# Query products between the tiles of the first stage: an order of instructions on three engines is changed

## What is computed

```python
def layernorm(x): return (x - mean(x)) / sqrt(var(x) + 1e-5)

# attention with a summed key-value product
h = layernorm_wb(layernorm(X))
Q, K, V = split(h @ W_in + b_in, 3)              # W_in: 512 x 1536
Q, K = rope_half(Q), rope_half(K)                # first 256 features rotated
A = sum over tokens of (K / norm(K)) * V         # one row of 512 per batch
x = X + layernorm(((A * Q) @ W_out + b_out) + layernorm(X))

# feed-forward: 2 of 8 experts per token, and a shared one
n = layernorm(x)
routed = sum over the token's top 2 of gate * (gelu(n @ w1[e] + b1[e]) @ w2[e] + b2[e])
shared = gelu(n @ shared_w1 + shared_b1) @ shared_w2 + shared_b2
out = x + layernorm(routed + shared)
```

## Time and profile before

| | |
|---|---|
| time, median of 3 runs | 949.71 us (947.07 to 954.91) |
| time of the profiled execution | 945.85 us |
| its span, first to last instruction | 944.0 us |
| TensorE (PE) busy | 93% of the span |
| VectorE (DVE) busy | 67% |
| ScalarE (ACT) busy | 46% |
| GpSimd (POOL) busy | 41% |
| granted TensorE clock, mean | 0.984 of 2.4 GHz |
| first stage, first product of group 1 to `sum_acc(1)` | 54.47 to 305.53 us |

### The profile page before, as it was taken

How to read it: one execution, slowest core, us unless ns; L and a number is a source line. 1 busy time by engine, 2 the same in 40 slices (tenths; PEclk the granted TensorE clock), 3 DMA queues, 4 the chain that set the end, 5 groups by cost and what they waited for, 6 DMA issues and landing times.

```text
span 944.0 us, 14783 instructions
## 1 busy us (share of the span) xinstructions
PE 879.7 (93%) x4558; PEld 724.0 (77%) x4558; DVE 636.5 (67%) x1370; ACT 436.1 (46%) x829; POOL 390.0 (41%) x321
## 2 busy tenths in 40 slices
PE   4999999999999989999999987799999999998986
PEld 3788777877888667777877776688888888886865
DVE  6866976966966765666656587366665556564877
ACT  5235445245243142241222544366666666664564
POOL 1456557366454000000000000467777567762175
PEclk9999999999999999999999998799999999999998
DMA  8327977878558895568433889497888878787999
GB/s 302 113 92 263 333 253 263 318 261 312 212 194 332 343 340 217 200 235 288 150 112 120 331 333 274 102 234 138 148 148 165 202 145 164 149 132 179 360 190 212
DMA packets 87626, 209.03 MB, mean 221 GB/s; under 512 B 11496, under 2 KB 19944, under 8 KB 82432
## 3 DMA queue, kind: packets, MB, share of 16 engines
q1 hardware_dynamic: 62592, 162.29, 47.5%
q0 software_dynamic: 19360, 43.60, 25.2%
q10 hardware_dynamic: 5600, 2.20, 1.0%
HBM read 117.05 MB, written 91.01 MB: 220 GB/s over the span
## 4 chain that ended last, share of the span: by engine, by line
PE 47%; DVE 10%; issue 10%; ACT 4%; POOL 3%; DMA 2%; DVEq 0%; POOLq 0%; ACTq 0%
PE bank L1822 3%; PE bank L1807 3%; PE bank L1820 3%; PE bank L1821 3%; PE bank L1837 3%; PE bank L1578 3%; PE bank L1839 3%; PE bank L1838 3%; PE bank L1579 3%; PE bank L1580 3%; PE bank L1829 2%; PE bank L1573 2%; PE bank L1728 2%; PE bank L1729 2%; PE bank L1730 2%
## 5 line engine op out<-in xcount | busy, mean ns | idle before, releaser
L1527 POOL DMA_INDIRECT f_scratch<-ro,dst x71 | 112.5, 1585 | 56.9 <-issue 19.8
L1519 POOL DMA_INDIRECT xr<-n_scratch,ids x71 | 70.1, 987 | 75.8 <-issue 54.8
L1578 PE MATMUL bank<-wkv_hi,h_hi 128*128 128x512 f32 x248 | 97.2, 392 | 0.0
L1580 PE MATMUL bank<-wkv_hi,h_lo 128*128 128x512 f32 x248 | 96.6, 389 | 0.0
L1579 PE MATMUL bank<-wkv_lo,h_hi 128*128 128x512 f32 x248 | 96.5, 389 | 0.0
L1319 DVE TENSOR_TENSOR ro<-bank,b2b 128x512 f32<-128x512 f32 x71 | 49.2, 692 | 68.3 <-PE bank L1839 55.4
L1820 PE MATMUL bank<-we,x_hi 128*128 x284 | 86.0, 303 | 0.3 <-DVE x_lo L1299 0.3
L1822 PE MATMUL bank<-we,x_lo 128*128 x284 | 80.5, 283 | 0.0
L1821 PE MATMUL bank<-we,x_hi 128*128 x284 | 80.3, 283 | 0.0
L633 ACT ACTIVATE sq<-kb 128x512 f32<-128x512 f32 x32 | 20.3, 633 | 125.8 <-DVE kb L946 125.8
L1837 PE MATMUL bank<-we,g_hi 128*128 x142 | 56.8, 400 | 3.2 <-DVE g_lo L1311 2.3
(11 more groups left out here) (242 smaller groups left out, 2523.6 us busy)
## 6 DMA issues: line engine op xcount, KB each, us to landing
xg<-in_X SPq DMA_DIRECT2D x15, 1024.0 KB, 7.9
we<-expert_scratch SPq DMA_DIRECT2D x6, 2048.0 KB, 13.1
w_lo<-in_w SPq DMA_DIRECT2D x16, 512.0 KB, 5.3
expert_scratch<-w_hi SPq DMA_DIRECT2D x16, 512.0 KB, 2.9
expert_scratch<-w_lo SPq DMA_DIRECT2D x16, 512.0 KB, 4.2
q_scratch<-qh SPq DMA_DIRECT2D x8, 1024.0 KB, 3.9
q_scratch<-qb SPq DMA_DIRECT2D x8, 1024.0 KB, 6.1
q_hi<-q_scratch SPq DMA_DIRECT2D x8, 1024.0 KB, 4.8
```

Of the source, the lines that this page charges most:

```text
L1519: pool.indirect_dma_start(xr[u][:, :], None, n3_dram, bass.IndirectOffsetOnAxis(ids[:, i:i + 1], 0)).then_inc(row_in[u], 16)
L1527: pool.indirect_dma_start(f_dram, bass.IndirectOffsetOnAxis(dst[:, i:i + 1], 0), ro[i % NRO][:, :], None, compute_op=ALU.add).then_inc(r_s ...
L1578: pe.matmul(dst, hi(k), w_hi(k), start=(k == 0), stop=False)
L1580: last = pe.matmul(dst, lo(k), w_hi(k), start=False, stop=(k == KD - 1 and not more))
```

## The change

Groups 1 to 7 get a new order; group 0 keeps the old one.

- TensorE: `q(g, j)` stands behind the keys and values of tile j. Both `turn` pairs of the next group stand around `q(g, 2)`, so ahead of the fourth tile.
- ScalarE: `bias_q(g, (j,))` stands in the loop over tiles, behind `norm_k(g, j)` and a `unit_hi` for each tile. `front_split` of all four slices stands behind the third tile's bias.
- GpSimd: `q_times_sin` and `front_lo(g + 1)` stand ahead of the fourth tile's `rnorm` and the last two accumulates.
- The lists of VectorE and SyncE are as before.

```diff
@@ bias_q
-                    if m in (1, 2):
-                        unit_hi_in(g, 1 + m)
@@ ScalarE
                     norm_k(g, j)
                     if j == 1 and g >= 1:
                         q_hi_parts(g - 1)
-                    if j % 2 == 0:
-                        unit_hi_in(g, j // 2)
-                if g + 1 < NG:
-                    front_split(g + 1, (g + 1) % 2, (0, 1))
-                    bias_q(g, (0,))
-                    front_split(g + 1, (g + 1) % 2, (2, 3))
-                    bias_q(g, (1, 2, 3))
+                    unit_hi_in(g, j)
+                    if g >= 1:
+                        bias_q(g, (j,))
+                        if j == 2 and g + 1 < NG:
+                            front_split(g + 1, (g + 1) % 2)
+                if g == 0:
+                    front_split(1, 1, (0, 1))
+                    bias_q(0, (0,))
+                    front_split(1, 1, (2, 3))
+                    bias_q(0, (1, 2, 3))
@@
-            act.wait_ge(tp_full, KD * NG)
-            bias_q(NG - 1)
             q_hi_parts(NG - 1)
@@ GpSimd
-                rnorm(g, 3)
-                accumulate(g, 2)
-                accumulate(g, 3)
-                if g + 1 < NG:
-                    front_lo(g + 1)
-                q_times_sin(g)
+                if g == 0:
+                    rnorm(g, 3)
+                    accumulate(g, 2)
+                    accumulate(g, 3)
+                    front_lo(1)
+                    q_times_sin(0)
+                else:
+                    q_times_sin(g)
+                    if g + 1 < NG:
+                        front_lo(g + 1)
+                    rnorm(g, 3)
+                    accumulate(g, 2)
+                    accumulate(g, 3)
@@ TensorE
                 for j in range(GT):
                     kv(g, j, 0)
-                    if j == GT - 1 and g + 1 < NG:
+                    if g == 0 and j == GT - 1:
+                        turn(1, (0, 1))
+                    kv(g, j, 1)
+                    if g == 0:
+                        continue
+                    if j == 2 and g + 1 < NG:
                         turn(g + 1, (0, 1))
-                    kv(g, j, 1)
+                    q(g, j)
+                    if j == 2 and g + 1 < NG:
+                        turn(g + 1, (2, 3))
                 if g == 0:
+
                     pe.wait_ge(w_split, 3 * KD)
-                for m in range(KD):
-                    q(g, m)
-                    if m == 0 and g + 1 < NG:
-                        turn(g + 1, (2, 3))
+                    for m in range(KD):
+                        q(g, m)
+                        if m == 0:
+                            turn(1, (2, 3))
```

## The result

The changed kernel takes 966.36 us (964.40 to 968.24, median of 4) where the kernel before takes 948.39 on the same occasions: a ratio of 1.0186, 95% interval 1.0152 to 1.0220. It is slower by 18 us; the forecast was 6.1 slower, 955.8, and its range ended at 965. The profiled executions differ by as much: 964.40 against 945.85.

The account below looks back on a forecast made before the run. TensorE, busy 93% of the span, was taken as the bound. Six groups at 37.04 plus 0.81, 32.65 and 1.5 give 257.2 us against 251.06: 949.7 + 6.1 = 955.8 us, range 948 to 965.

Parts of the forecast that it names:

- Query products between the tiles: First stage: each query buffer is asked for again after three or more products, so the 5.1 us bias wait goes.
- The second turned pair: Ahead of the fourth tile TensorE waits for ScalarE's read-out of rows 0 and 1: 2.62 us in each of six groups.
- The clock, rival C: A product behind each of six holds runs at 1.2 GHz, 2.72 us more each: +16 on top, 972; chance 0.03.
- Weight units: ScalarE's third unit is through at T+23.8, ahead of bias_q(g, 2) at 25.57; inside the sum it costs nothing.
- rival A: Weight loads decide through a VectorE, SyncE and ScalarE loop of 35.3 to 37.0, or 39 with collisions: 964; chance 0.16.
- End of the stage: Before sum_acc(1), one query product instead of four follows the last keys and values: 1.4 us wait, 0.1 restart.
- Rival B: The second turned pair finds its banks free, so groups take 34.42: -9.6 us, 940; chance 0.05.

Follow-up runs that it names:

- experiment 4: The changed kernel with group 7 alone back in the old order (four keys-and-values tiles, then four query products) on three engines: 960.12 us, ratio 1.0120.
- experiment 1: The changed kernel with nine extra matmuls a group, result overwritten, filling TensorE's waits around the second turned pair: 961.48 us, ratio 1.0135.
- experiment 3: The changed kernel with the third weight unit's high part moved on ScalarE behind the bias and all four rows' read-out: 963.88 us, ratio 1.0155.
- experiment 2: The changed kernel with the next group's first two rows read out on ScalarE ahead of the third weight unit and bias: 949.00 us, ratio 1.0004.
- experiment 5: The kernel of experiment 2 with the fourth weight unit's high part moved on ScalarE behind the fourth bias and the acol copy: 945.13 us, ratio 0.9951.
- experiment 7: The changed kernel with TensorE's second turned pair moved from behind q(g, 2) to behind kv(g, 3, 0): 950.01 us, ratio 1.0019.

## Why the prediction was wrong

The path was right and its size was not: +6.1 forecast, +18.0 measured. By its steps:

*Query products between the tiles.* Right: no wait for `q_free` in groups 1 to 4 and 6. But the step overlooked that `sum_acc(0)` takes a query bank in turn. Between `q(4, 3)` and `q(5, 0)`, which then share a bank, stand two large products and not three or more.

*The second turned pair.* Right in place and in size: 2.62 worked out; group 1, where nothing else happened, took 37.08 for 37.04, and without the hold two groups took 34.45 and 34.43 for 34.42.

*The clock, rival C.* This is the step that failed most: the cost of a fall of the clock behind the holds stood in the sum at nothing. It had a chance of 0.03 because "the old gaps of 1.1 and 0.7 left the granted clock at 1.00". Those are single gaps of at most 1.1; the hold has 2.2 us of idle with 0.6 of transposes between. (Whether the sum or the 1.54 alone matters, no run separates.) Four falls behind holds and one behind the last accumulate: the first product behind the four took 3.43, 4.41, 4.42 and 3.93 where 2.84 was forecast, 4.8 together. With 0.7 for the slowed transposes of groups 2 and 6, and the 1.3 by which the stages behind are longer, it is 6.8 in the profile (behind the fifth fall the first product takes 4.21, and 2.96 in experiment 4, which has no fall there); experiment 1 measures 4.9 less in the median. The price was wrong too, at 2.72 for each of six. Five of twelve holds of exactly 1.54 and 0.67 (in the changed kernel and experiments 3 and 4) have a fall behind them, and one costs 0.9 to 1.6. The kernel before had a comparable hold all along, in group 0 (idle 1.45 and 0.61 at 43.90 and 45.14), the same in every kernel here. The window of 40 to 50 us, before and in experiment 2:

```profile
40.00:50.00 10.00, 7.94 (x39) 6.18 (x38) 5.27 (x8) 5.65 (x10) 7.02 (x7) 1.00 0.36 133
```
```profile
40.00:50.00 10.00, 7.93 (x33) 6.16 (x32) 5.38 (x8) 5.57 (x10) 7.02 (x8) 0.83 0.39 140
```

Unchanged code, and one execution has the fall and the other hasn't; of the ten profiles six have it and four don't. A single profile with a clock of 1.00 doesn't show that an idle time is free.

*Weight units.* "Inside the sum it costs nothing" failed as a term. The slack was 1.8 us. The loads landed later than 5.2 (median 6.2 in this stage of the changed kernel), and in group 2 VectorE came to `k_tile(1)` at T+12.7 instead of T+11.1. In group 2 ScalarE waits for it with the bias behind it:

```profile
118.00 1.06 ACT L677 ACTIVATE w_hi<-w_lo 128x1024 fp32r<-128x1024 f32 x1 [3.46 <-DMA w_lo<-in_w]
118.97 0.67 ACT L646 ACTIVATE qb<-bank,bq 128x512 f32<-128x512 f32 x1
```

That put 0.9, 0.2 and 1.1 on the holds of groups 2, 3 and 4 (2.45, 1.78 and 2.64 instead of 1.54), 2.3 together; experiment 3, without them, is 2.5 faster in the median, which agrees but, at its scatter, doesn't fix the size. It is rival A's queue, but not rival A: no loop set the period. Of the fourth unit's wait the prediction said that "queued behind it is only `bias_q(g, 3)`, wanted at T'+22.6". That time is wrong: with two banks in turn it is wanted at T'+13.6, by `q(g + 1, 1)`, which costs nothing, and in group 4 at T'+5.4, by `q(5, 0)`, which started at T'+6.7 and was itself 0.15 slower. That is 1.4. The recorded expectation of experiment 5 calls the waiting product the second of group 5 and the releaser the copy; it is the first, and the bias. The edit moves the unit behind both, so its result stands.

*End of the stage.* Right in kind, 2.2 and a restart instead of 1.4 and 0.1. The product row took 1.77 as allowed for, but the last accumulate 2.18 where the earlier trace rows had 1.29:

```profile
320.59 2.18 POOL L1453 TENSOR_TENSOR acc<-acc,prod 128x512 f32<-128x512 f32 x1 [0.63 <-DVE prod L958]
```
```profile
320.43 1.21 DVE L965 TENSOR_TENSOR rc<-qb,rf 128x1024 f32<-128x1024 f32 x1
```

The rotation that used to wait for the query bias now stands right behind the product on VectorE and runs at the same time; the accumulate ends 1.13 behind it. By the rule of the Trainium skill that rival A names (page "SBUF — State Buffer", section "SBUF: two separate sides") that is a wait of 1.05 and then a run of 1.13; the rows come near it, as an accumulate alone takes 1.29.

The account: 6.1 forecast and found, 2.3 weight units, 1.4 the wait of `q(5, 0)`, 0.9 the last accumulate, 6.8 the clock, and 0.9 by which group 1 already starts later (55.39 against 54.47) though group 0 is unchanged; over the ten profiles that start lies between 54.5 and 55.7. That makes 18.4 of 18.6 in the profile.

*Two sums* are off, and nothing rests on them: the rows hold 11.1 us over 34.42 in groups 1 to 6, not some 10, and the lower bound is +4.0, not +3.7 (six holds 0.22 shorter and an end 0.8 shorter than in the +6.1).

*Rival B.* The hold was called unavoidable: "two queues in order, each naming the other's product". Right for this order, and experiments 2 and 7 show that one move on either queue is enough.

## What to carry to other kernels

When two engines' lists are interleaved, lay both out against each other instruction by instruction: a read-out queued behind the bias of product n makes the turn that needs it wait for product n, whatever else is ready. An idle TensorE costs more than its idle time where a fall of the clock may follow; count a hold with all its idle times (that their sum is what matters isn't shown), and give the fall a chance even if one profile shows none. A wait on a load costs whatever stands behind it in that queue; when banks go in turn, an extra user in one group shifts who waits for whom. A view's releaser is inferred, so check its end against the start of what waited.

## What the runs showed of the hardware

- Idle times of 1.54 and 0.67 us with 0.63 of transposes between them let TensorE's granted clock fall to 1.2 GHz for 3.4 us in 5 of 12 cases and not in 7. With 1.44 to 1.49 and 0.61 in group 0 it fell in 6 of 10 profiles, and with 1.03 and 0.67 in one case (experiment 7). Filled down to 0.3 us or less, or up to 0.8 where a weight load was late, none fell in that execution.
- A fall costs 0.9 to 1.6 us of dense products, less than the 1.7 that half speed over 3.4 us would make, when it begins while the engine still idles.
- A GpSimd accumulate took 2.18 instead of 1.29 beside a VectorE multiply with two inputs in SBUF, and ended 1.13 behind it.
